# Routed experts' factors moved from the tokens to the silu, on GpSimd

## The reference

```python
g = einsum('bsd,edf->ebsf', x, Wg);  u = einsum('bsd,edf->ebsf', x, Wu)
expert_outs = einsum('ebsf,efd->ebsd', silu(g) * u, Wd)
expert_output = einsum('be,ebsd->bsd', gates, expert_outs)
shared = einsum('bsf,fd->bsd', silu(x @ Sg) * (x @ Su), Sd)
out = x + (1 - sg) * expert_output + sg * shared        # gates: (8, 8), sg: one factor for each batch
```

## Time and profile before

| | us |
|---|---|
| Median of 3 runs (156.59 to 157.03) | 156.63 |
| The profiled execution | 156.61 |
| Its span, first to last instruction | 155.3 |
| Outside the span | 1.31 |
| PE busy | 152.2 (98%) |
| ACT busy | 108.9 (70%) |
| DVE busy | 98.6 (63%) |
| POOL busy | 77.4 (50%) |

### The profile page before, as it was taken

The page is one execution under the profiler, slowest core; times in us unless marked ns, Lnnn a source line. Parts: engine busy times, 40 slices in busy tenths (PEclk is TensorE's granted clock), DMA queues, the critical chain, the costliest instruction groups (busy, mean ns, idle before and its releaser), DMA issues.

```text
span 155.3 us, 2306 instructions
## 1 busy us (share of the span) xinstructions
PE 152.2 (98%) x673; PEld 124.3 (80%) x673; DVE 98.6 (63%) x160; ACT 108.9 (70%) x204; POOL 77.4 (50%) x78
## 2 busy tenths in 40 slices
PE   7999999999999999999999999999999999999993
PEld 2888888888888888888888888888888888888873
DVE  0597677765666666666666666666665666666692
ACT  4877876776687757775778577766776687755541
POOL 1758993547255645546354825572547255650000
PEclk9999999999999999999999999999999999999999
DMA  4975015004100330005000500070000000000006
GB/s 145 254 177 176 0 21 186 0 2 168 36 0 0 101 108 0 0 27 175 0 0 0 203 0 0 0 186 16 0 0 0 0 0 0 0 0 4 0 0 135
DMA packets 12727, 8.24 MB, mean 53 GB/s; under 512 B 5041, under 2 KB 10673, under 8 KB 12721
## 3 DMA queue, kind: packets, MB, share of 16 engines
q1 hardware_dynamic: 12144, 7.64, 17.8%
q10 hardware_dynamic: 576, 0.52, 1.0%
HBM read 7.64 MB, written 0.52 MB: 53 GB/s over the span
## 4 chain that ended last, share of the span: by engine, by line
PE 98%; ACT 0%; issue 0%
PE y_ps L519 10%; PE y_ps L521 10%; PE y_ps L528 10%; PE u_ps L639 9%; PE g_ps L634 9%; PE g_ps L635 9%; PE u_ps L640 9%; PE u_ps L641 9%; PE g_ps L636 9%; PE u_ps L507 2%; PE u_ps L600 1%; PE g_ps L588 1%; PE g_ps L591 1%; PE u_ps L602 1%; PE u_ps L599 1%; PE g_ps L586 1%
## 5 line engine op out<-in xcount | busy, mean ns | idle before, releaser
L431 DVE TENSOR_TENSOR h_ps<-silu,u_ps 128x512 f32<-128x512 f32 x71 | 49.2, 696 | 49.0 <-PE u_ps L641 44.6
L345 ACT ACTIVATE h_hi<-h_ps 128x512 fp32r<-128x512 f32 x71 | 42.5, 599 | 38.3 <-DVE h_ps L431 38.3
L251 POOL TENSOR_TENSOR w_lo<-w_raw,w_hi 128x384 fp32r<-128x384 f32 x32 | 32.5, 1016 | 38.3 <-ACT w_hi L335 38.2
L436 DVE TENSOR_TENSOR h_lo<-h_ps,h_hi 128x512 fp32r<-128x512 f32 x71 | 48.4, 683 | 0.1
L340 ACT ACTIVATE silu<-g_ps 128x512 f32<-128x512 f32 x72 | 42.8, 597 | 0.2 <-PE g_ps L565 0.2
L256 POOL TENSOR_TENSOR xs_lo<-xs,xs_hi 128x512 fp32r<-128x512 f32 x16 | 20.6, 1290 | 15.8 <-ACT xs_hi L331 15.8
L528 PE MATMUL y_ps<-h_lo,w_hi 128*128 128x512 f32 x71 | 27.6, 389 | 0.0
L521 PE MATMUL y_ps<-h_hi,w_hi 128*128 128x512 f32 x71 | 27.6, 389 | 0.0
L519 PE MATMUL y_ps<-h_hi,w_lo 128*128 128x512 f32 x71 | 27.6, 389 | 0.0
L634 PE MATMUL g_ps<-x_hi,w_hi 128*128 128x512 f32 x64 | 24.9, 389 | 0.0
L635 PE MATMUL g_ps<-x_lo,w_hi 128*128 128x512 f32 x64 | 24.9, 389 | 0.0
(11 more groups left out here) (81 smaller groups left out, 118.7 us busy)
## 6 DMA issues: line engine op xcount, KB each, us to landing
w_raw<-in_L_cond_Wg SPq DMA_DIRECT2D x8, 256.0 KB, 2.9
w_raw<-in_L_cond_Wu SPq DMA_DIRECT2D x8, 256.0 KB, 3.4
w_raw<-in_L_cond_Wd SPq DMA_DIRECT2D x8, 256.0 KB, 3.8
x_nat<-in_x SPq DMA_DIRECT2D x2, 128.0 KB, 2.9
w_raw<-in_L_cond_Su ACTq DMA_DIRECT2D x2, 128.0 KB, 3.4
w_raw<-in_L_cond_Sd SPq DMA_DIRECT2D x1, 256.0 KB, 4.1
x_blk<-in_x SPq DMA_DIRECT2D x4, 64.0 KB, 3.1
out<-y_blk SPq DMA_DIRECT2D x4, 64.0 KB, 2.2
```

The costliest lines, as they stand in the source:

```text
L345: act.activation(h_hi[k % HB][:, :], h_ps[k % BANKS][:, :], ACT.Copy)\
L431: dve.tensor_tensor((to or h_ps[k % BANKS])[:, :], silu[k % BANKS][:, :], u_ps[k % BANKS][:, :], ALU.mult).then_inc(hidden_done, 1)
L436: dve.tensor_tensor(h_lo[k % HB][:, :], h_ps[k % BANKS][:, :], f32(h_hi[k % HB][:, :]), ALU.subtract).then_inc(h_lo_done, 1)
```

## The change

- The tokens are no longer scaled: `xs`, its two split copies, and their operations on ScalarE (line 331) and GpSimd (lines 246, 256) go. The up projection reads x_hi and x_lo, as the gate does.
- GpSimd copies the expert's factors to a small tile, waits for that copy, and then multiplies each unit's silu by them in place, 64 times. VectorE's `hidden` of a routed unit waits for this product and no longer for ScalarE's silu.
- ScalarE's order in routed units becomes silu of unit k+1, hidden_hi of unit k, then a weight slice if k is 2, 4, 5 or 6.
- VectorE's order in routed units becomes hidden_lo of unit k-1, then hidden of unit k.
- GpSimd subtracts a slice's lower part after scaling the unit that follows it. The two additions to base_t now stand between the seventh and the eighth routed expert.
- The last unit is scaled and multiplied in two halves of 256 columns, and the third `natural` waits for the second half.

```diff
-    PREPARE = [("slice", 0), ("half", 0)] + [("slice", n) for n in range(1, NF)] + [("half", 1)]
+    SPLIT_AT = [2, 4, 5, 6]
...
+            def scale(buf, k, n, pieces=1):
+                h = k // NF
+                c = factor[buf][:, h * HBATCH:(h + 1) * HBATCH]
+                pool.wait_ge(silu_done, n + 1)
+                for i in range(pieces):
+                    some = slice(i * NQ // pieces, (i + 1) * NQ // pieces)
+                    t = tokens(silu[k % BANKS][:, :])[:, some, :, :]
+                    by = c.unsqueeze(1).unsqueeze(3).to_broadcast([P, NQ // pieces, HBATCH, PER])
+                    pool.tensor_tensor(t, t, by, ALU.mult).then_inc(scaled, 1)
+
+            def routed(e, buf, nxt=None):
+                pool.tensor_copy(factor[buf][:, :], coef[:, e - 1, :]).then_inc(factor_copied, 1)
+                pool.wait_ge(factor_copied, e)
+                for k in range(UNITS):
+                    last = nxt is None and k == UNITS - 1
+                    scale(buf, k, UNITS * e + k, 2 if last else 1)
+                    if nxt is not None and k - 1 in SPLIT_AT:
+                        slice_lo(SPLIT_AT.index(k - 1), *nxt)
+
+            for n in range(NF):
+                slice_lo(n, 1, 0)
             pool.wait_ge(coef_ready, 1)
+            with pool.Fori(0, E // 2 - 1) as i:
+                for q in range(2):
+                    routed(2 * i + 1 + q, 1 - q, (q, 2 * NF * i + NF * (q + 1)))
+            routed(E - 1, 1, (0, NF * (E - 1)))
+
             pool.wait_ge(x_t_done, len(PIECES))
             pool.wait_ge(x1_turned, 1)
...
             for h in range(HALVES):
                 pool.wait_ge(base_scaled, h + 1)
                 pool.tensor_tensor(base_t[:, h, :], base_t[:, h, :], x_t[:, h, :], ALU.add)\
                     .then_inc(base_done, 1)
+
+            routed(E, 0)
...
             def routed_units(base, nxt):
                 for k in range(UNITS):
-                    silu_of(base + k, k)
+                    if nxt is not None or k < UNITS - 1:
+                        silu_of(base + k + 1, (k + 1) % UNITS)
+                        hidden_hi(base + k, k)
                     if nxt is not None and k == LAG:
                         act.wait_ge(down_done, base)
-                    if nxt is not None and k >= LAG:
+                    if nxt is not None:
                         split_next(k, *nxt)
-                    if nxt is not None or k < UNITS - 1:
-                        hidden_hi(base + k, k)
...
+            silu_of(UNITS, 0)
...
-            def hidden(n, k, first=False, to=None):
-                dve.wait_ge(silu_done, n + 1)
+            def hidden(n, k, first=False, routed=False):
+                if routed:
+                    dve.wait_ge(scaled, n - UNITS + 1)
+                else:
+                    dve.wait_ge(silu_done, n + 1)
                 dve.wait_ge(up_done, n + 1)
...
             with dve.Fori(2, E) as e:
                 for k in range(UNITS):
-                    hidden(UNITS * e + k, k)
                     hidden_lo(UNITS * e + k - 1, (k - 1) % UNITS)
+                    hidden(UNITS * e + k, k, routed=True)
...
             hidden_lo(LAST - 1, UNITS - 2)
-            hidden(LAST, UNITS - 1, to=h_last)
+            dve.wait_ge(up_done, LAST + 1)
+            for i in range(2):
+                cols = slice(i * HALF_N, (i + 1) * HALF_N)
+                dve.wait_ge(scaled, LAST - UNITS + 1 + i)
+                dve.tensor_tensor(h_last[:, cols], silu[(UNITS - 1) % BANKS][:, cols],
+                                  u_ps[(UNITS - 1) % BANKS][:, cols], ALU.mult).then_inc(hidden_done, 1)
...
-                    if f == 0:
-                        pe.wait_ge(xs_lo_done, halves_before + h + 1)
...
-                    pe.matmul(u[:, :], hi, xs_hi[buf][:, h, :], start=True, stop=False)
-                    pe.matmul(u[:, :], hi, xs_lo[buf][:, h, :], start=False, stop=False)
-                    pe.matmul(u[:, :], lo, xs_hi[buf][:, h, :], start=False, stop=True)\
+                    pe.matmul(u[:, :], hi, x_hi[:, h, :], start=True, stop=False)
+                    pe.matmul(u[:, :], hi, x_lo[:, h, :], start=False, stop=False)
+                    pe.matmul(u[:, :], lo, x_hi[:, h, :], start=False, stop=True)\
                       .then_inc(up_done, 1)
```

More of the change, by code:

```diff
@@ L42, in build @@
     LAST = (E + 1) * UNITS - 1
-    PREPARE = [("slice", 0), ("half", 0)] + [("slice", n) for n in range(1, NF)] + [("half", 1)]
-    FIRST_PREPARE = [("slice", 0), ("slice", 1), ("half", 0), ("slice", 2), ("half", 1), ("slice", 3)]
+    SPLIT_AT = [2, 4, 5, 6]
     assert E % 2 == 0 and NF == 4 and UNITS % HB == 0 and UNITS % BANKS == 0 and NQ == 4
-    assert LAG == BANKS and HB > LAG and UNITS == LAG + len(PREPARE)
+    assert LAG == BANKS and HB > LAG
     ctx = ExitStack()
@@ L80, in build @@
         coef = sbuf("coef", [P, E + 1, B], FP32)
+        factor = [sbuf(f"factor{i}", [P, B], FP32) for i in range(2)]
         ident = sbuf("ident", [P, P], FP32)
@@ L126, in build @@
         base_done = sem("base_done")
-        xs_done = sem("xs_done")
-        xs_hi_done = sem("xs_hi_done")
-        xs_lo_done = sem("xs_lo_done")
+        scaled = sem("scaled")
+        factor_copied = sem("factor_copied")
         w_hi_done = sem("w_hi_done")
@@ L242, in gpsimd_program @@
                 .then_inc(second_x_lo, 1)
[L244 to L247, removed]
             def slice_lo(n, buf, slices_before):
@@ L252, in slice_lo @@
                                    f32(w_hi[buf][:, :, n, :]), ALU.subtract).then_inc(w_lo_done, 1)
[L254 to L269, removed]
@@ L281, in gpsimd_program @@
[L281 to L287, removed]
             for h in range(HALVES):
@@ L346, in hidden_hi, with split_next @@
                    .then_inc(h_hi_done, 1)
[L348 to L353, removed]
+            def split_next(k, buf, loads):
+                if k in SPLIT_AT:
+                    w_hi_slice(SPLIT_AT.index(k), buf, loads)
             def routed_units(base, nxt):
                 for k in range(UNITS):
-                    silu_of(base + k, k)
+                    if nxt is not None or k < UNITS - 1:
+                        silu_of(base + k + 1, (k + 1) % UNITS)
+                        hidden_hi(base + k, k)
                     if nxt is not None and k == LAG:
                         act.wait_ge(down_done, base)
-                    if nxt is not None and k >= LAG:
+                    if nxt is not None:
                         split_next(k, *nxt)
-                    if nxt is not None or k < UNITS - 1:
-                        hidden_hi(base + k, k)
             for k in range(BANKS):
@@ L430, in hidden @@
                     dve.wait_ge(h_lo_done, n - BANKS + 1)
-                dve.tensor_tensor((to or h_ps[k % BANKS])[:, :], silu[k % BANKS][:, :], u_ps[k % BANKS][:, :],
+                dve.tensor_tensor(h_ps[k % BANKS][:, :], silu[k % BANKS][:, :], u_ps[k % BANKS][:, :],
                                   ALU.mult).then_inc(hidden_done, 1)
@@ L472, in vector_program @@
             for k in range(UNITS):
-                hidden(UNITS + k, k)
                 hidden_lo(UNITS + k - 1, (k - 1) % UNITS)
+                hidden(UNITS + k, k, routed=True)
                 if k == 0:
@@ L480, in vector_program @@
                 for k in range(UNITS):
-                    hidden(UNITS * e + k, k)
                     hidden_lo(UNITS * e + k - 1, (k - 1) % UNITS)
+                    hidden(UNITS * e + k, k, routed=True)
             for k in range(UNITS - 1):
-                hidden(UNITS * E + k, k)
                 hidden_lo(UNITS * E + k - 1, (k - 1) % UNITS)
+                hidden(UNITS * E + k, k, routed=True)
                 if k == NF + 1:
@@ L622, in tensor_program, with routed_expert @@
                 down(k - LAG, k - LAG, 0, begin=(k - LAG) % NF == 0)
-            def routed_expert(base, buf, halves_before, slices_before, first=False):
+            def routed_expert(base, buf, slices_before, first=False):
                 for k in range(UNITS):
@@ L647, in routed_expert @@
                     down(base + k - LAG, (k - LAG) % UNITS, buf if k >= LAG else 1 - buf, begin=begin)
[L649 removed]
+            routed_expert(UNITS, 1, 0, first=True)
             with pe.Fori(0, MID) as i:
                 for q in range(2):
[L652 to L654 removed]
+                    routed_expert(2 * UNITS * i + UNITS * (q + 2), q, 2 * NF * i + NF * (q + 1))
+            routed_expert(E * UNITS, 0, NF * (E - 1))
             down(LAST - 1, UNITS - 2, 0)
@@ L670, in tensor_program @@
             natural(1)
+            pe.wait_ge(hidden_done, LAST + 2)
             natural(2)
```

24 lines of the change are left out of this document (6 added, 18 removed).

## The result

The changed kernel takes 159.42 us (median of 4 runs, 159.03 to 160.02), the kernel before 156.83 in the same comparison (156.59 to 157.13): ratio 1.0178, 95% interval 1.0156 to 1.020. It is 2.6 us slower. In a later comparison one execution of the kernel before took 258.39 us at a mean granted clock of 0.56; it is counted in none of the ratios. The profiled execution took 159.09 with a span of 157.8, against 156.61 and 155.3.

A forecast was written before the change was run, and what follows sets the result against it. TensorE, busy 98% of the span, was taken to bound the kernel. Terms 0 + 1.85 (stop) + 0.82 (end) = 2.67 us on the profiled 156.61 gave 159.3 (72%), range 158.3 to 161.4.

The forecast's parts named there:

- The stop: Before the last routed expert: base_t additions delay unit 64's scaling, TensorE stops 1.85 us, mostly at unit 66's up matmuls.
- The sign named: TensorE idle once, some 1.6 us before unit 66's up matmul near 139, and about 0.2 before a down matmul.
- The loop of hidden, hidden_hi, hidden_lo: Between VectorE and ScalarE: one turn 1.95 us against TensorE's 2.04 a unit, so lateness shrinks 0.09 a unit.
- Rival B: VectorE-ScalarE loop slower than 2.04, say 2.10 a turn: sum 6.0 us, time 162.6; chance 10%.
- The end: Last units: remaining lateness of hidden delays unit 70's third down matmul (L528) and everything behind it by 0.82 us.
- its floor of 0.44: At the end, with no lateness from the additions, L528 of unit 70 would still cost 0.44 us.
- The expert boundaries: At each change of expert the factors' copy puts hidden at 2.95, inside 3.60, gone in four units: cost 0.
- the limit of 3.60: Latest start of hidden, counted from its unit's start, that costs TensorE nothing; steady value 2.62, so 0.98 us slack.
- The load: SyncE's load after the fourth lower slice lands about 91.8, ScalarE wants it at 93.5: hidden by 1.7.
- Rival A: GpSimd's in-place scaling costs 1.29 like two full tiles: sum 4.8 us, time 161.4; chance 8%.
- Rival C: TensorE's 1.85 us stop lowers its clock, adding 1.5, the end getting 0.38 back: 160.4; chance 6%.
- Rival D: The base_t additions before unit 64's scaling don't hold TensorE up, only the end's 0.44 remains: 157.0; chance 4%.

The follow-up runs named there:

- small_op_psum: adds_late plus, behind each routed unit's hidden_lo, a 128-column VectorE subtraction with one operand in the accumulation memory: 165.25 us (one run).
- no_scale: The changed kernel without the 65 multiplications by the factor, hidden waiting for silu, additions left between the experts: 157.24 us, ratio 1.0035 to the kernel before.
- old_act: adds_late with ScalarE's old order in routed units (silu, slice, hidden_hi of the same unit): 224.57 us (one run).
- old_act_last_wait: old_act with hidden's wait for the scaled silu written last, behind its other waits: 217.91 us (one run).
- adds_late: The changed kernel with both additions to base_t moved into the last routed expert, behind the scalings of units k = 1 and 3: 157.05 us, ratio 1.0023 to the kernel before.
- small_op: adds_late plus a 128-column VectorE copy between hidden_lo and hidden in each routed unit: 206.72 us (one run).
- old_dve: adds_late with VectorE's old order in routed units, hidden of unit k before hidden_lo of unit k-1: 169.96 us (one run).

## Why the prediction was right, step by step

It said 159.3 and 2.67 us more; 159.42 and 2.59 came out, and the forecast's mechanism is the one that the runs show.

- **The stop.** Predicted: hidden of unit 64 starts 5.45 after its unit, 1.85 are lost. The trace: unit 64 starts at 134.11, hidden at 139.54, 5.43; 1.78 lost. Two terms inside were off and cancelled: copy and wait took 0.26 (138.20 to 138.46) and not 0.40, and GpSimd came free for the additions 0.12 later, at 3.63 instead of 3.51. The 0.07 between 1.85 and 1.78 is the weight load, of which a late operand exposes 0.11 and not 0.19. The sign named was some 1.6 us before the up matmul of unit 66 and about 0.2 before a down matmul. The up matmul comes 1.42 late (140.29 for 138.87) and exposes 0.11, 1.53 in all, of which the view counts 1.25 as idle; the rest is lost at the down matmul L519, 141.64.
- **The loop of hidden, hidden_hi, hidden_lo.** Predicted 1.95 a turn. It is 1.96 (0.73, 0.63 and 0.60 for the terms) wherever hidden is late (139.54, 141.50, 143.46 and so on to 149.34 and 151.30 in VectorE's timeline). Rival B is out; small_op_psum shows how it would have looked.
- **The end.** Predicted 0.82, measured 0.84, and here too terms cancelled. Hidden of unit 70 came 1.13 after unit 71's start and not 1.02, as the stop leaves hidden 3.65 after its unit (5.43 less 1.78) and not 3.60, and a turn wins back 0.08 and not 0.09; against that stands the weight load's 0.08 again. Most of the loss is at the first down matmul of unit 70, which waits for hidden_hi (152.67 and its exposed load, 0.57); the third adds 0.27. The working had put it all at the third. And I laid its floor of 0.44 on the scaling; no_scale showed that ScalarE's new order with VectorE's makes it (0.36) without any scaling.
- **The expert boundaries** cost TensorE nothing, as predicted, but not as I described them. I had hidden back at 2.62 after four units. In VectorE's loop it never comes back but stays between 2.79 and 3.20: at a boundary and behind it, in the changed kernel's timeline of VectorE,

```profile
36.78 0.70 DVE L416 TENSOR_TENSOR h_ps<-silu,u_ps 128x512 f32<-128x512 f32 x1
...
39.27 0.70 DVE L416 TENSOR_TENSOR h_ps<-silu,u_ps 128x512 f32<-128x512 f32 x1 [0.39 <-POOL silu L253]
...
41.24 0.69 DVE L416 TENSOR_TENSOR h_ps<-silu,u_ps 128x512 f32<-128x512 f32 x1
```

  units 15, 16 and 17, the distance is 2.49 and then 1.97; unit 19 starts at 42.31 and its hidden at 45.16, 2.85 later. The step that failed is the scaling to hidden, priced 1.08 from a row outside any loop; in the loop it is 1.23 to 1.25 when the scaling comes last. That this cost nothing is owed to the slack and not to the working: 3.20 is still 0.4 under the limit of 3.60. In old_act the same 0.15 was paid in every unit of the loop (3.12 for 2.97).
- **The other terms.** The head gained the 0.04 (units 2 to 8 take 12.24, 19.87 less 7.63). The load was hidden: ScalarE never sat idle before a weight slice (L318, 0.0 us in 32). GpSimd is busy 107.3 us, as worked out; ScalarE 101.9 and not 99, which cost nothing and whose cause was not looked for.
- **Rival A** is out: the scaling in place took 1.04 as a whole unit (63 of the 65; two are the last unit's halves), like the one of the tokens, and less than the 1.11 estimated from the Trainium skill (GPSIMD Engine Reference, section 3.1).
- **Rival C** is out: the granted clock is 1.00 from 137 to 143 us, and behind the stop the matmuls follow each other at 0.23. This stop, 1.25 us of idle time, did not lower the clock. The Trainium skill (TensorE: Matmul & The Clock Gate, Part 1) says that idleness lowers it. This stop was not enough, but old_act shows the fall, in TensorE's timeline at its end:

```profile
216.48 0.50 PE L511 MATMUL y_ps<-h_hi,w_lo 128*128 128x512 f32 x1 [1.74 <-ACT h_hi L331]
...
218.19 1.19 PE L650 MATMUL g_ps<-w_raw,h_last 128*128 128x128 f32 x4 [0.48 <-DVE h_last L486]
```

  TensorE had idled about 0.5 us in each unit at a granted clock of 1.00, then 1.74 and, from 217.71, 0.48. From 218.3 to 221.6 the granted clock is 0.50, the lower of its two levels, and four matmuls of 128 columns take 1.19 instead of 0.70 (153.73 in the changed kernel). In old_act_last_wait, which idled 1.84 at the same place, the clock stayed at 1.00 until the last matmul was done.
- **Rival D** did not come by itself, but adds_late built it: 157.05 against the 157.0 that it was given.

## What to carry to other kernels

An engine at 68% can still be the one that stops the kernel: what counts is which operation stands ahead of which in its queue, and how much slack the waiting chain has. Work that nobody waits for goes where the queue has a gap that fits it, in pieces, and not as a block ahead of work that is waited for; here 2.5 us in one block stopped TensorE for 1.8 us and made the end 0.5 longer, and the same in two pieces cost nothing. Before reordering two engines against each other, add up the loop between them start to start: it may leave a few hundredths of a microsecond where their busy shares promise a third of the time.

## What the runs showed of the hardware

- A copy on VectorE from one tile of the main memory to another (128 columns, small_op) didn't run beside a GpSimd operation but ended 0.08 to 0.09 us after it, 59 times out of 59: 0.22 us alone, 0.95 in the median of all 63; an operation that reads the accumulation memory and one tile kept its 0.28 (small_op_psum, all 64 between 0.280 and 0.283). The Trainium skill (SBUF — State Buffer, Who interferes with whom) says so: copies in a two-port mode and GpSimd share a port pair that one holds for a whole instruction. The trace agrees.
- It counts which instruction carries the wait that ends last (old_act, old_act_last_wait). VectorE's product started 0.03 after GpSimd's end where it carried the wait itself, 0.13 where one semaphore instruction ahead of it did, and 0.19 where a register instruction did and a semaphore instruction followed. The written order of the waits moved this both ways, so the trace has to be looked at after such an edit.
- An operand that came late to a matmul cost 0.05 of hand-over and 0.11 of its weight load of 0.19 (old_dve, 82.07 to 82.47; the changed kernel, 141.59 to 141.98).
